# Another order of ScalarE, TensorE and VectorE where attention ends and feed-forward begins, and the last batch's rows in a dead token buffer

## The reference

```python
q = jax.nn.softmax(q, axis=-1); k = jax.nn.softmax(k, axis=-2)
state = jnp.einsum('bhnd,bhne->bhde', k, v)
out = jnp.einsum('bhnd,bhde->bhne', q, state)
out = layer_norm(out) @ Wo.T + bo
x = _layernorm(x + out, axis=-1)
h = layer_norm(x, ln1_g, ln1_b)
h = jax.nn.gelu(h @ ternary(w1).T + b1, approximate=False)
h = layer_norm(h, ln2_g, ln2_b)
x = _layernorm(x + h @ ternary(w2).T + b2, axis=-1)
```

## Time and profile before

| | us |
|---|---|
| three runs, median (lowest to highest) | 569.5 (569.3 to 569.98) |
| the profiled execution | 569.85 |
| its span | 568.0 |
| PE busy in the span | 541.4 |
| DVE, ACT, POOL busy | 502.9, 483.1, 402.7 |

### The profile page before, as it was taken

How to read it: one execution, slowest core, us unless ns; L and a number is a source line. 1 busy time by engine, 2 the same in 40 slices (tenths; PEclk the granted TensorE clock), 3 DMA queues, 4 the chain that set the end, 5 groups by cost and what they waited for, 6 DMA issues and landing times.

```text
span 568.0 us, 10876 instructions
## 1 busy us (share of the span) xinstructions
PE 541.4 (95%) x3542; PEld 494.0 (87%) x3542; DVE 502.9 (89%) x1276; ACT 483.1 (85%) x951; POOL 402.7 (71%) x390
## 2 busy tenths in 40 slices
PE   6999999999999999988899999999999999999990
PEld 6899999898999989878788998888899888899890
DVE  5888898988899898857587999999999999999986
ACT  4655689799989878877989999999999999999983
POOL 4782979877797987575458776876676776675672
PEclk9999999999999999999999999999999999999996
DMA  8540040230705020250111012222112222100102
GB/s 294 198 149 2 1 186 39 82 141 9 289 1 224 1 113 38 76 200 24 75 38 39 38 37 76 75 74 76 44 33 75 76 74 76 59 18 37 39 38 111
DMA packets 11399, 46.52 MB, mean 82 GB/s; under 512 B 1360, under 2 KB 1744, under 8 KB 9168
## 3 DMA queue, kind: packets, MB, share of 16 engines
q1 hardware_dynamic: 10912, 45.29, 21.9%
q10 hardware_dynamic: 432, 0.54, 0.3%
HBM read 29.02 MB, written 16.81 MB: 81 GB/s over the span
## 4 chain that ended last, share of the span: by engine, by line
PE 74%; DVE 11%; ACT 8%; DMA 2%; issue 2%; POOL 1%; ACTq 0%; DVEq 0%; POOLq 0%
PE ring L1874 20%; PE qps_sps_aps_then_y L1898 20%; PE qps_sps_aps_then_y L1745 7%; PE qps_sps_aps_then_y L1659 7%; PE ring L1687 5%; PE qps_sps_aps_then_y L1764 5%; PE ring L1816 2%; DVE z L1177 2%; PE ring L1791 2%; DVE qsum L1071 1%; PE ring L1779 1%; PE ring L1829 1%; PE qps_sps_aps_then_y L1720 1%; ACT z L746 1%; DMA w_raw<-in_wq_dram 1%
## 5 line engine op out<-in xcount | busy, mean ns | idle before, releaser
L1898 PE MATMUL qps_sps_aps_then_y<-ff_w_over_xc_lo,ff_a_lo_over_qw 128*128 128x258 f32 x512 | 126.5, 283 | 0.0
L1898 PE MATMUL qps_sps_aps_then_y<-ff_w_over_xc_lo,ff_a_hi_over_xc_lo 128*128 128x258 f32 x512 | 126.4, 283 | 0.0
L1874 PE MATMUL ring<-ff_ht_hi_over_qw,t 128*128 128x512 f32 x256 | 105.6, 412 | 0.9 <-DVE ff_ht_lo_over_xc_hi L1249 0.5
L1874 PE MATMUL ring<-ff_ht_lo_over_xc_hi,t 128*128 128x512 f32 x256 | 100.8, 394 | 0.0
L1898 PEld LDWEIGHTS qps_sps_aps_then_y<-ff_w_over_xc_lo,ff_a_hi_over_xc_lo 128*128 128x128 f32 x512 | 96.9, 189 | 3.5
L1898 PEld LDWEIGHTS qps_sps_aps_then_y<-ff_w_over_xc_lo,ff_a_lo_over_qw 128*128 128x128 f32 x512 | 96.7, 189 | 3.4
L1257 DVE SCALAR_TENSOR_TENSOR ff_a_lo_over_qw<-ring,ff_rho,ff_a_hi_over_xc_lo 128x512 fp32r<-128x512 f32 x128 | 91.5, 742 | 5.7 <-ACT ff_a_hi_over_xc_lo L807 4.5
L789 ACT ACTIVATE ring<-ring,bias 128x512 f32<-128x512 f32 x128 | 84.1, 677 | 11.2 <-PE ring L1874 10.2
L522 POOL TENSOR_TENSOR ff_accp_over_xt_lo<-ff_accp_over_xt_lo,ff_sq_over_ek_et_hi 128x512 f32<-128x512 f32 x64 | 84.3, 1317 | 4.7
L805 ACT ACTIVATE ff_sq_over_ek_et_hi<-ring 128x512 f32<-128x512 f32 x128 | 79.1, 618 | 0.5
L807 ACT CAST ff_a_hi_over_xc_lo<-ring 128x512 fp32r<-128x512 f32 x128 | 78.0, 609 | 0.0
(11 more groups left out here) (179 smaller groups left out, 1631.1 us busy)
## 6 DMA issues: line engine op xcount, KB each, us to landing
x_scratch<-z SPq DMA_DIRECT2D x16, 514.0 KB, 2.9
ff_x_over_w_raw_xc<-x_scratch SPq DMA_DIRECT2D x16, 514.0 KB, 4.8
xt<-in_x_tok_dram SPq DMA_DIRECT2D x8, 1024.0 KB, 4.8
out_dram<-ff_z_over_et_lo SPq DMA_DIRECT2D x15, 512.0 KB, 3.5
xc<-in_x_chan_dram SPq DMA_DIRECT2D x6, 1024.0 KB, 6.9
w_raw<-in_w_dram SPq DMA_DIRECT2D x2, 1024.0 KB, 5.4
xc<-in_x_chan_dram SPq DMA_DIRECT2D x2, 512.0 KB, 6.7
ek<-in_x_chan_dram SPq DMA_DIRECT2D x1, 1024.0 KB, 9.3
```

The lines of the kernel that those rows point to most:

```text
L1874: mm = nc.tensor.matmul(ff_bank(k, m), t1[:, c, m * P:(m + 1) * P], h[:, k % 2, c], start=(c == 0 and j == 0), stop=(c == CH - 1 and j == 1))
L1898: last = nc.tensor.matmul(ff_yps[:, t, 0:C + 2], a[:, m % DEPTH, t * P:(t + 1) * P], ff_w2[:, m], start=(m == 0 and j == 0), stop=(m == FC ...
```

## The change

Nothing is added to or taken from what is computed, but for one ScalarE instruction on one column (a Gelu whose result isn't used). Five things differ.

1. ScalarE does `k_exponent(7, 0)` before `projected_high(6)` instead of behind `normalise(5, 1)`. PE does `ternary_bias` behind `state_project(6)`, and VectorE `folded_bias` behind `projected_low(6)`.
2. `scale_w2` takes a first and a last number and is called four times for two of its eight instructions, between the high halves of batch 7. `product_out(6, 5)` stands before `et_high(7, 1)`.
3. The one-column Gelu stands before `state_copy(7)`, and with it the table load, which stood at the first `ff_gelu`.
4. `squares(6, 1)` goes behind `ff_ht_high(0, 1)` and `state_out(7)`, `normalise(6, 1)` behind the first two Gelus. `ff_first(0, 2)` comes before `attend(7, 0)`, no longer behind `attend(7, 1)`.
5. The rows of batch 7 go into `z_last`, which is `xt[0]`, and their variance into a tile `last_var` of its own. `product_out(7, 0)` waits for the residuals of batch 6, no longer for its stores. Stores and loads of batch 7's rows leave out the variance column, so that they move 256 of 257 columns.

```diff
+        z_last = xt[:, NB % 2]
+
+        def z_rows(b):
+            return z_last if b == NB - 1 else z[:, :, 0:C]
...
+                    if b < NB - 1:
+                        sp.dma_start(x1_scratch[b, :, gs], z[:, gs]).then_inc(x1_out, 16)
+                    else:
+                        sp.dma_start(x1_scratch[b, :, gs, 0:C], z_last[:, gs]).then_inc(x1_out, 16)
 
             def ff_load(k):
-                sp.dma_start(ff_x1[:, k % XB], x1_scratch[k // 2, :, (k % 2) * TB:(k % 2 + 1) * TB]
+                n = C if k // 2 == NB - 1 else C + 1
+                sp.dma_start(ff_x1[:, k % XB, :, 0:n], x1_scratch[k // 2, :, (k % 2) * TB:(k % 2 + 1) * TB, 0:n]
...
                 if t == 0:
-                    wait_for(act, x1_out, 16 * NG * b)
+                    if b < NB - 1:
+                        wait_for(act, x1_out, 16 * NG * b)
+                    else:
+                        act.wait_ge(z_ok, T * b)
                 act.wait_ge(a_stat, T * b + t + 1)
-                nc.scalar.copy(z[:, t, 0:C], a_bank(b, t)[:, P:P + C]).then_inc(y_out, 1)
+                nc.scalar.copy(z_rows(b)[:, t], a_bank(b, t)[:, P:P + C]).then_inc(y_out, 1)
...
-            def scale_w2():
-                act.wait_ge(ff_g_step, 1)
-                act.wait_ge(f_tern, 8)
-                for m in range(FC):
+            def scale_w2(first, last):
+                if first == 0:
+                    act.wait_ge(ff_g_step, 1)
+                    act.wait_ge(f_tern, 8)
+                for m in range(first, last):
...
             normalise(NB - 3, 0)
+            k_exponent(NB - 1, 0)
             projected_high(NB - 2)
             normalise(NB - 3, 1)
-            k_exponent(NB - 1, 0)
...
             product_out(NB - 2, 4)
+            scale_w2(0, 2)
             et_high(NB - 1, 0)
+            product_out(NB - 2, 5)
+            scale_w2(2, 4)
             et_high(NB - 1, 1)
-            product_out(NB - 2, 5)
+            scale_w2(4, 6)
             pt_high(NB - 1, 2)
             pt_high(NB - 1, 3)
+            scale_w2(6, 8)
...
             product_out(NB - 2, 7)
-            scale_w2()
-            act.wait_ge(ff_gain_ok, 1)
+            act.wait_ge(half_ok, 6)
+            nc.scalar.activation(spark[:], nhalf[:, 0:1], ACT.Gelu)
             state_copy(NB - 1)
             squares(NB - 2, 0)
-            squares(NB - 2, 1)
             ff_ht_high(0, 1)
             state_out(NB - 1)
+            squares(NB - 2, 1)
             normalise(NB - 2, 0)
             projected_high(NB - 1)
-            normalise(NB - 2, 1)
             ff_gelu(0, 0)
             ff_gelu(0, 1)
+            normalise(NB - 2, 1)
             product_out(NB - 1, 0)
...
             projected(NB - 2)
+            projected_low(NB - 2)
             folded_bias()
-            projected_low(NB - 2)
...
             state_transpose(NB - 2)
-            ternary_bias()
             k_product(NB - 1, 1, 0)
             state_project(NB - 2)
+            ternary_bias()
...
             ff_first(0, 1)
+            ff_first(0, 2)
             attend(NB - 1, 0)
             ff_transposes(1, 0)
             attend(NB - 1, 1)
-            ff_first(0, 2)
             attend(NB - 1, 2)
```

More of the change, by code:

```diff
@@ L156, in both_halves @@
         fence = sb("fence", [P, 1])
+        last_var = sb("last_var", [P, T])
         tern_bias = sb("tern_bias", [P, 3])
@@ L469, in norm_rstd @@
                 pool.wait_ge(z_fin, 4 * n - 1)
[L470 removed]
+                var = last_var[:, gs] if b == NB - 1 else z[:, gs, C]
+                nc.gpsimd.tensor_tensor(var, vaZ[:, gs], eps[:, gs], ALU.add).then_inc(z_fin, 1)
             def ternary_round(n, first):
@@ L483, in ff_norm_rstd @@
                 wait_for(pool, ff_n_ok, TB * k)
-                nc.gpsimd.tensor_tensor(ff_rs1[:], ff_x1[:, k % XB, :, C], nhalf[:, 0:TB], ALU.pow).then_inc(ff_n_rstd, 1)
+                var = ff_x1[:, k % XB, :, C]
+                if k // 2 == NB - 1:
+                    pool.wait_ge(z_fin, 4 * NG * NB)
+                    var = last_var[:, (k % 2) * TB:(k % 2 + 1) * TB]
+                nc.gpsimd.tensor_tensor(ff_rs1[:], var, nhalf[:, 0:TB], ALU.pow).then_inc(ff_n_rstd, 1)
             def ff_hidden_rstd(k):
@@ L1177, in residual @@
                     nc.vector.scalar_tensor_tensor(
-                        out=z[:, t, 0:C], in0=z[:, t, 0:C], scalar=rsA[:, t:t + 1],
+                        out=z_rows(b)[:, t], in0=z_rows(b)[:, t], scalar=rsA[:, t:t + 1],
                         in1=xt[:, b % 2, t], op0=ALU.mult, op1=ALU.add, accum_out=zsum[:, t:t + 1]).then_inc(z_ok, 1)
```

9 lines of the change are left out of this document (4 added, 5 removed).

## The result

The changed kernel took 566.64 us (median of 4 runs, 566.29 to 567.33), the kernel before, beside it, 569.74 us (569.3 to 570.56): ratio 0.9945, with a 95% interval of 0.993 to 0.9961. A second comparison with more runs of the kernel before gave 567.01 us against 569.79, ratio 0.9957 (0.9944 to 0.9969). The forecast was 567.1, range 566.2 to 568.6, and faster. Its chain of steps was a gain of 2.43 us; measured where it lies, the gain is 2.46 us.

The account below looks back on a forecast made before the run. PE was taken as the bound, full from 330 to 548 us, so starting that stretch earlier ends the kernel earlier. 1.06, 0.94 and 0.43 make 2.43 us, from the median of 569.5 to 567.1 us; range 566.2 to 568.6.

Parts of the forecast that it names:

- Step 1: ScalarE, batch 6: k_exponent(7, 0) fills a gap, so r_hi of batch 6 comes 0.54 us earlier.
- Step 2: Batch 7's high halves: scale_w2 in ScalarE's gaps, product_out(6, 5) earlier; transposes ahead of the sums 1.14 us earlier.
- Step 3: ScalarE's copy of xe starts 1.66 us earlier; the one-column Gelu costs nothing, with 1.4 us to spare.
- Step 4: From xe to r_hi of batch 7: ScalarE's new order brings r_hi at 273.58, 1.06 us earlier.
- Step 5: Batch 7's rows in xt: attend(7, 2) 2.43 us earlier (1.06, 0.94 of ff_first(0, 2), 0.43 of waiting).
- Step 6: Batch 7's stores and loads in 1,024-byte pieces: taken as costing nothing, with 4.6 us covered before block 5.
- (c): Slower by batch 7's transfers: 8.7 us more landing, of which 4.6 are covered, 571.2 us; chance 0.05.
- (a): Half of it: r_hi of batch 7 isn't advanced, 0.94 + 0.43 stay, 568.1 us; chance 0.10.
- (b): Given back: feed-forward's start (290 to 305 us) is bound by something not earlier, 569.5 us; chance 0.10.
- (d): PE's clock falls in the 1.7 us idle before attend(7, 0): 4.2 us more, 571.3 us; chance 0.03.

Follow-up runs that it names:

- e7: The changed kernel with k_exponent(7, 0), ternary_bias and folded_bias back in their old places; 567.46 us.
- e3: The changed kernel without the one-column Gelu, so that the table load falls to feed-forward's first Gelu; 569.21 us.
- e2: The changed kernel with scale_w2's eight instructions in one block again, behind product_out(6, 7); 569.36 us.
- e4: The changed kernel with ff_first(0, 2) behind attend(7, 1) again; 569.55 us.
- e1: The changed kernel with batch 7's rows back in z, so product_out(7, 0) waits for batch 6's stores again; 570.43 us.
- e8: The changed kernel with ff_first(0, 2) back behind attend(7, 1) and ff_transposes(1, 0) moved ahead of attend(7, 0); 568.84 us.
- e9: The changed kernel with r_hi of batch 7 ahead of normalise(6, 0) and normalise(6, 1) behind product_out(7, 1); 567.45 us.
- e12: The kernel of e9 with normalise(6, 1) cut up and its pieces put into ScalarE's gaps; 566.31 us, ratio 0.994 to the kernel before.

## Why the prediction was right, and where it was not

**Step 1** had the times right and the worth wrong. r_hi of batch 6 was forecast for 242.87, and came at 241.61 + 1.26 = 242.87. The cover for a late attend(6, 0) was real but thin: it came at 244.95 + 1.26 = 246.21, where I had 245.85; r_lo took 1.24 us instead of the usual 0.96, ternary_rows waited 1.45 us for the folded bias (243.94), and the chain of after runs through r_lo and it. And the 0.54 us that I carried on was no term of the sum in the end: by e7 the whole part is worth 0.10.

**Step 2** had the right mechanism and too small a gain. attend(6, 7) came at 255.20 + 1.26 = 256.46 for 256.30 by the chain (254.95, so 256.21, in the timeline), with no idle before it. The eight transposes and what follows the sums, before and then after:

```profile
261.25 1.04 PE L1791 MATMUL ring<-ident,ek 128*128 128x128 f32 x8
266.44 0.60 PE L1816 MATMUL ring<-ident,ff_xn 128*128 128x128 f32 x4
```

```profile
258.40 1.04 PE L1815 MATMUL ring<-ident,ek 128*128 128x128 f32 x8
263.58 0.60 PE L1840 MATMUL ring<-ident,ff_xn 128*128 128x128 f32 x4
```

The transposes start at 258.40 + 1.26 = 259.66 instead of 261.25, so 1.59 us earlier and not 1.14. The 261.86 of the earlier trace rows, where the forecast started, is the end of the first four of them; after, these end at 258.57 + 0.44 = 259.01 in the chain, which is 260.27 and not the forecast 260.72. I had VectorE's low half of pt(7, 3) hold them back; it was through by 258.67 + 1.26 = 259.93, and PE came to the transposes without an idle.

**Step 3**: xe came at 265.04 (263.78 + 1.26), 0.45 earlier than the 265.49. That is step 2's 0.45: from the start of the transposes to the end of the sums PE took as long as before (263.58 - 258.40 = 5.18 us, and 266.44 - 261.25 = 5.19). The cover of the table load and the one-column Gelu was 1.02 us where I counted 1.4. The one-column Gelu took 0.20, and followed the load by 0.02 us. The Trainium skill ("ScalarE: Activation LUTs", What ACT_TABLE_LOAD costs) adds a drain of 1.38 us to the load; the profiled executions of the changed kernel and of e3, where the load stands on the path and costs 1.06 us, don't show it.

**Step 4** is where most of that 0.45 went. `st` came at 269.22 for 269.37, r_hi of batch 7 at 273.44 for 273.58, straight behind the four normalisations. Both are within 0.15, but the wait in front of `st` I had left to the chain by way of xe alone. It belongs to VectorE's residual(6) too: e2 and e7 delay xe by 2.00 and 0.31, and `st` only by 1.69 and 0.11.

**Step 5** held: attend(7, 0) at 275.31 for 275.46, its idle 1.44 for 1.7, attend(7, 2) at 276.69 + 1.26 = 277.95 for 278.11, and no store in the chain. All three are 0.15 to 0.26 better than forecast, and 0.13 of that was given back on the way to the transposes; that the sum and the measured gain agree to 0.03 us is in part luck. The split of the 2.43 into 1.06, 0.94 and 0.43 is an account along one path, and taking parts away doesn't give it back: undoing one costs 3.77, 1.70, 1.06, 2.31 or 0.10 us, 8.9 together for a gain of 2.46. Each holds up the same attend, and in the profiled executions two of them the clock.

**Step 6** put the transfers at nothing, and that came true for a wrong reason. The two stores in small pieces land in 5.5 us (median) instead of 2.9, so pieces do cost, 2.6 us for each store; the earlier trace rows had suggested otherwise. DMA issues of after (count, KB each, median us), and GpSimd:

```profile
x_scratch<-xt SPq DMA_DIRECT2D x2, 512.0 KB, 5.5
```

```profile
330.46 1.02 POOL L499 TENSOR_TENSOR ff_rs<-ff_x_over_w_raw_xc,nhalf 128x4 f32<-128x4 f32 x1 [0.85 <-DMA ff_x_over_w_raw_xc<-x_scratch]
334.13 2.35 POOL L524 TENSOR_TENSOR ff_x1c_over_xt_hi<-ff_x_over_w_raw_xc,ff_c_row 128x512 f32<-128x512 f32 x2 [2.65 <-DVE ff_z_over_et_lo L1344]
```

GpSimd's ff_rs now waits 0.85 us for the load of block 5, which it didn't before. I had named that as a sign of being wrong, and it came, but it cost nothing: GpSimd still idles 2.65 us for VectorE behind it. Rival (c)'s cover of 4.6 us is what held, with 2.65 left.

**The rivals.** (a), half of it, did not happen: r_hi of batch 7 came 1.20 us earlier by distance (272.18 - 238.54 against 274.64 - 239.80). (b), given back: 2.59 at attend(7, 2), 2.46 at the transposes, and from there to the end the profiled pair loses 0.16 us more (264.59 and 264.75). (c) fell by its cover. (d) did not happen at an idle of 1.44 us, nor, by their mean clocks of 0.990 to 0.993, in any of the nine executions of the changed kernel, but I had priced it at 0.03 on a bad argument. The 3.43 us of idle between 5 and 14 us, with 1.00 in the column of the clock, were to show that idle doesn't lower it. PE's timeline of the kernel before speaks against that reading:

```profile
13.97 0.41 PE L1659 MATMUL qps_sps_aps_then_y<-w_lo,xc_hi 128*128 128x256 f32 x1
...
15.44 0.28 PE L1659 MATMUL qps_sps_aps_then_y<-w_hi,xc_lo 128*128 128x256 f32 x1
```

Matmuls of 256 columns stand 0.21 us apart from 9.5 to 14.4 us and 0.12 us from 15.0 on: about half the pace, for 23 of them. It is nearly the ratio of e4 (0.32 and 0.17), where the column did show the fall; that it is the clock here too is inferred from this, not shown. In the changed kernel's profiled execution only 12 are slow, up to 11.5 us: 11 x 0.09 = 1.0 us less, and its first matmul starts 0.38 us earlier (8.76 for 9.14). That covers the 1.26 us by which the pair differs ahead of the changed code, and no edit touches it. The Trainium skill ("TensorE: Matmul & The Clock Gate", Part 1) lets the clock fall when the array idles: the profiled executions of e1 and e4 agree, at 2.38 and 2.39 us. The shorter idles of the other profiled executions, up to 2.25 us, did not lower it, but by the mean clocks of e2 and e8 idles of 2.25 and 1.95 us probably did in others.

So the chance of 0.03 was too low. Had the change left ff_first(0, 2) where it was, the prediction's own sum would have put its idle at 2.6 us and the time 0.94 above the forecast, and e4 shows 2.31. The sum holds since the move that fills the idle is part of the change; that this also kept the clock was luck, for the forecast counted the move as work only.

## What to carry to other kernels

Measure a change of a microsecond as a distance within the trace, between a landmark in front of the changed code and the start of the stretch that is bound, not by totals: the start of this kernel alone varies by more than the gain. When several moves shorten one chain, ask for each new idle of the bound engine how long it becomes, and put ready work into it even if that work is needed only later: in e4 the clock cost more than the 0.94 us of work that would have filled the idle. Don't take one profile for all executions there; at about 2 us of idle a profile showed the good case and most of the times the other. And a block that is moved back to free one instruction must be cut to the size of the gaps it goes into: e9 and e12 differ in that alone, by 1.9 us of distance.
